# A second group norm in two chains of two channel blocks each, placed among the projection and Gram matmuls

## The reference

```python
hn = group_norm(x, gn1_scale, gn1_bias)              # 32 groups of 16 channels
... # layer 0: 8 heads of attention over 1024 positions -> a
out = jnp.einsum('bchw,oc->bohw', a, w_proj) + b_proj[None, :, None, None]
out = group_norm(out, gn2_scale, gn2_bias)
x1 = x + out                                          # input of layer 1
...
qkv = jnp.einsum('oc,bcn->bon', w_qkv, x1)            # weight-normed
rms = jnp.sqrt(jnp.mean(jnp.square(qkv), axis=1, keepdims=True)) + 0.0001
q, k, v = jnp.split(qkv / rms, 3, axis=1)
attn = softmax(einsum('bci,bcj->bij', q, k) * C ** (-0.5))
h = einsum('oc,bcn->bon', w_out, einsum('bij,bcj->bci', attn, v))
return (x1 + h) * 2.0 ** (-0.5)
```

## Time and profile before

| what | value |
|---|---|
| runs, median (lowest to highest) | 3598.97 us (3598.38 to 3599.15) |
| span of the profiled execution | 3596.4 us |
| mean granted TensorE clock in it | 0.984 |
| busy: TensorE, DVE, ScalarE, GpSimd | 97%, 59%, 51%, 28% |
| chain that ended last: TensorE, issue, DVE, ScalarE, GpSimd | 86%, 7%, 3%, 2%, 1% |

### The profile page before, as it was taken

How to read it: one execution, slowest core, us unless ns; L and a number is a source line. 1 busy time by engine, 2 the same in 40 slices (tenths; PEclk the granted TensorE clock), 3 DMA queues, 4 the chain that set the end, 5 groups by cost and what they waited for, 6 DMA issues and landing times.

```text
span 3596.4 us, 52422 instructions
## 1 busy us (share of the span) xinstructions
PE 3475.9 (97%) x17296; PEld 2845.8 (79%) x17296; DVE 2104.1 (59%) x3363; ACT 1828.4 (51%) x3082; POOL 994.2 (28%) x891
## 2 busy tenths in 40 slices
PE   7999999989999899998999989999999999999999
PEld 3887788878888788887878878788787887888878
DVE  4677446774378634786347854478444774447742
ACT  3577226761278522784237832388223882247812
POOL 0234103440034300352114521045111451114411
PEclk9999999999999999999999999999999999999999
DMA  7622215312234113331033211342203422142210
GB/s 278 180 45 65 91 38 139 78 41 82 65 112 95 48 59 95 86 91 71 36 118 83 71 71 42 112 95 60 82 36 106 95 60 82 39 135 62 59 47 24
DMA packets 63519, 294.41 MB, mean 82 GB/s; under 512 B 9200, under 2 KB 9456, under 8 KB 52464
## 3 DMA queue, kind: packets, MB, share of 16 engines
q1 hardware_dynamic: 63216, 290.65, 27.6%
HBM read 158.49 MB, written 31.46 MB: 53 GB/s over the span
## 4 chain that ended last, share of the span: by engine, by line
PE 86%; issue 7%; DVE 3%; ACT 2%; POOL 1%; DMA 0%; ACTq 0%; SPq 0%; DVEq 0%; POOLq 0%
PE big L419 36%; PE tps L516 14%; PE big L543 12%; PE ops L529 12%; PE ops L658 10%; DVE XA L1163 1%; PE ops L419 1%; ACT PB L784 1%; PE big L581 1%; POOL XA L912 1%; DVE HL L1284 0%; DVE small L1104 0%; PE big L635 0%; PE ops L624 0%; ACT RB L801 0%
## 5 line engine op out<-in xcount | busy, mean ns | idle before, releaser
L902 POOL TENSOR_SCALAR PB<-PB,small 128x1024 f32<-128x1024 f32 x576 | 647.9, 1125 | 1334.5 <-DVE small L1110 1328.6
L790 ACT ACTIVATE PT<-tps 128x512 fp32r<-128x512 f32 x1088 | 601.1, 597 | 249.4 <-PE tps L516 246.0
L1115 DVE TENSOR_TENSOR PT<-tps,PT 128x512 fp32r<-128x512 f32 x1088 | 692.7, 678 | 38.6 <-ACT PT L790 38.6
L419 PE MATMUL big<-HH,W 128*128 128x512 f32 x1856 | 618.2, 404 | 61.8 <-DVE HL L1284 56.5
L1104 DVE TENSOR_REDUCE small<-big 128x1 f32<-128x1024 f32 x512 | 624.7, 1220 | 62.5 <-PE big L543 59.2
L516 PE MATMUL tps<-ident,PB 128*128 128x128 f32 x4608 | 617.4, 275 | 8.4 <-DVE PT L1115 6.1
L516 PEld LDWEIGHTS tps<-ident,PB 128*128 128x128 f32 x4608 | 527.6, 140 | 122.0 <-DVE PT L1115 52.5
L784 ACT ACTIVATE PB<-big,small 128x1024 f32<-128x1024 f32 x512 | 572.2, 1117 | 73.1 <-DVE small L1104 70.2
L529 PE MATMUL ops<-PT,VT 128*128 128x512 f32 x2048 | 599.1, 414 | 0.0
L543 PE MATMUL big<-ST 128*128 128x512 f32 x2048 | 555.2, 393 | 10.9 <-ACT PB L784 10.9
L419 PEld LDWEIGHTS big<-HH,W 128*128 128x128 f32 x1856 | 361.8, 195 | 149.2 <-issue 70.9
(11 more groups left out here) (130 smaller groups left out, 3669.9 us busy)
## 6 DMA issues: line engine op xcount, KB each, us to landing
ST<-ST SPq DMA_DIRECT2D x384, 256.0 KB, 5.0
W<-d_qk SPq DMA_DIRECT2D x32, 1024.0 KB, 5.5
XA<-in_x SPq DMA_DIRECT2D x8, 2048.0 KB, 8.9
X<-in_x SPq DMA_DIRECT2D x8, 2048.0 KB, 10.4
W<-d_wp SPq DMA_DIRECT2D x8, 2048.0 KB, 12.1
W<-d_g SPq DMA_DIRECT2D x8, 2048.0 KB, 12.1
W<-d_m SPq DMA_DIRECT2D x8, 2048.0 KB, 7.8
W<-d_u SPq DMA_DIRECT2D x8, 2048.0 KB, 7.6
```

What stands on the lines that cost most here:

```text
L419: last = mm(dst, stat(sp_, k), mov(mp_, k), start=(i == 0), stop=(i == n - 1))
L790: act_fn(pt_slot(u, s)[:, 0, :], tps[n % 2][:], ACT.Copy).then_inc(s_pt_hi, 1)
L902: nc.gpsimd.tensor_scalar(PB[:, i, :], PB[:, i, :], rinv[:, i:i + 1], 1.0, ALU.mult, ALU.mult)\
L1115: V.tensor_tensor(pt_slot(u, s)[:, 1, :], tps[n % 2][:], pt_slot(u, s)[:, 0, :].bitcast(f32), ALU.subtract).then_inc(s_pt_ready, 1)
```

## The change

- Group norm 2 goes in two chains, of blocks 0 and 1 and of blocks 2 and 3. The first one's group matmuls stand inside projection 2 on TensorE (after 9 and after 15 of its 24 matmuls), the second one's inside Gram blocks 1 and 2. They write the small PSUM tiles tps, so "gna" and "gnb" of this norm leave `BIG`.
- DVE's, ScalarE's and GpSimd's programs are reordered to match: residual, high half, float32 copy and low half of a pair follow its chain, in whole blocks.
- GpSimd multiplies x by 1/sqrt(2) in place in four steps during attention (after steps 20, 23, 26, 29); gs2 is scaled once, and the scale disappears from the later steps.
- DVE makes the low half from XA, coefB and the high half, and no longer from GpSimd's copy.
- The Gram blocks are taken in pieces: what needs x1 blocks 0 and 1 first, then blocks 2 and 3. Three additions of products move from DVE to GpSimd.
- x1's blocks 0 and 1 go to ST, since HH and HL are still read by the projection; y's blocks go where there is room.

The core of the diff:

```diff
-BIG += [("proj", k) for k in range(KB)] + [("gna", 0), ("gnb", 0)] + [("g", k) for k in range(KB)]
+BIG += [("proj", k) for k in range(KB)] + [("g", k) for k in range(KB)]
+X_SCALE_STEPS = (20, 23, 26, 29)
...
-                    sp.wait_ge(s_xc_hi, (b + 1) * len(XC_PARTS))
+                    sp.wait_ge(s_xc_lo, (b + 1) * KB)
...
-                for o in (2, 3):
-                    project_out(released(("proj", o)), o, range(PAIRS)).then_inc(s_big_full, 1)
-                group_means(2 * b + 2, released(("gna", 0)), bp, s_big_full)
-                group_vars(2 * b + 2, released(("gnb", 0)), s_big_full)
+                t = released(("proj", 2))
+                project_out(t, 2, range(3), (0,))
+                gn2_means(0)
+                project_out(t, 2, [3], (0,))
+                project_out(t, 2, range(1), (1,))
+                gn2_vars(0)
+                project_out(t, 2, range(1, PAIRS), (1,)).then_inc(s_big_full, 1)
+                project_out(released(("proj", 3)), 3, range(PAIRS)).then_inc(s_big_full, 1)
...
-                for k in range(KB):
-                    from_x1("g", k, 0, range(k + 1))
+                x1_block(0)
+                from_x1(released(("g", 0)), 0, 0, (0,)).then_inc(s_big_full, 1)
+                t = released(("g", 1))
+                from_x1(t, 1, 0, (0,))
+                gn2_means(1)
+                x1_block(1)
+                from_x1(t, 1, 0, (1,)).then_inc(s_big_full, 1)
+                g2 = released(("g", 2))
+                from_x1(g2, 2, 0, (0,))
+                gn2_vars(1)
+                from_x1(g2, 2, 0, (1,))
+                g3 = released(("g", 3))
+                from_x1(g3, 3, 0, (0, 1))
+                x1_block(2)
+                from_x1(g2, 2, 0, (2,)).then_inc(s_big_full, 1)
+                from_x1(g3, 3, 0, (2,))
+                x1_block(3)
+                from_x1(g3, 3, 0, (3,)).then_inc(s_big_full, 1)
... ScalarE
+                out_f32(0)
+                out_f32(1)
+                xc_hi(0)
+                out_f32(2)
+                xc_hi(1)
+                out_f32(3)
+                xc_hi(2)
+                xc_hi(3)
... GpSimd
+                    nc.gpsimd.tensor_scalar(X[:, k, :], X[:, k, :], RES, 1.0, ALU.mult, ALU.mult)\
+                      .then_inc(s_x_scaled, 1)
...
+                for c in range(GN2_PARTS):
+                    rows = slice(2 * c, 2 * c + 2)
+                    group_rstd(GN_PER_BATCH * b + 2 + c, rows)
+                    pool.wait_ge(s_coef_b, b * GN2_PARTS + c + 1)
+                    for k in (2 * c, 2 * c + 1):
+                        pool.wait_ge(s_res_sum, b * KB + k + 1)
+                        nc.gpsimd.tensor_scalar(X[:, k, :], XA[:, k, :], 1.0, coefB[:, k:k + 1], ALU.mult, ALU.add)\
+                          .then_inc(s_xc_ready, 1)
+                for k in range(1, KB):
+                    pool.wait_ge(s_prod_ready, b * KB + k + 1)
+                    nc.gpsimd.tensor_tensor(PB[:, 4, :], PB[:, 4, :], PB[:, 4 + k, :], ALU.add)\
+                      .then_inc(s_prod_add if k < KB - 1 else s_prod_sum, 1)
... DVE
+                def xc_lo(k):
+                    dve.wait_ge(s_xc_hi, b * KB + k + 1)
+                    V.scalar_tensor_tensor(x1(1, k), XA[:, k, :], coefB[:, k:k + 1], x1(0, k).bitcast(f32),
+                                           ALU.add, ALU.subtract).then_inc(s_xc_lo, 1)
...
+                out_stats(0)
+                out_stats(1)
+                gn2_mean(0)
+                gn2_dev(0)
+                gn2_veps(0)
+                gn2_coefs(0)
+                residual(0)
+                out_stats(2)
+                residual(1)
+                xc_lo(0)
+                out_stats(3)
+                gn2_mean(1)
+                xc_lo(1)
+                gram_product(0)
+                gn2_dev(1)
+                gram_product(1)
+                gn2_veps(1)
+                gn2_coefs(1)
+                residual(2)
+                residual(3)
+                xc_lo(2)
+                xc_lo(3)
+                gram_product(2)
+                gram_product(3)
```

More of the change, by code:

```diff
@@ L74 @@
 BIG_BASE = SETUP_BIG
-DVE_LINKS = 16
+DVE_LINKS = 18
 SCALE0 = float(CH) ** -0.5
 SCALE1 = float(C) ** -0.5
-XC_PARTS = [(0, slice(0, HALF)), (0, slice(HALF, N))] + [(k, slice(0, N)) for k in range(1, KB)]
+GN2_PARTS = 2
+GN_PER_BATCH = GN2_PARTS + 1
+X_SCALE_STEPS = (20, 23, 26, 29)
 LAG = 5
@@ L571, in body, with project_out @@
                 pe.wait_ge(s_a_lo, b * 6 + 6)
-                def project_out(t, o, pairs):
-                    for half in range(2):
+                def project_out(t, o, pairs, halves=(0, 1)):
+                    for half in halves:
                         if o == 0 and pairs == [PAIRS - 1]:
@@ L599, in from_x1 @@
+                project_out(t, 2, range(3), (0,))
[5 more added lines that the diff above has]
+                project_out(released(("proj", 3)), 3, range(PAIRS)).then_inc(s_big_full, 1)
+                def from_x1(t, k, slot, blocks):
                     for half in range(2):
[L600 to L603, removed]
@@ L604, in from_x1 @@
                         cols = slice(HALF * half, HALF * half + HALF)
-                        last = split_product(t[:, cols], lambda h, j: w_full[slot][:, h, j, P * k:P * k + P],
-                                             lambda h, j: (HH, HL)[h][:, j, cols], blocks)
-                    last.then_inc(s_big_full, 1)
+                        for j in blocks:
+                            for i, (wp, xp) in enumerate(((0, 0), (0, 1), (1, 0))):
+                                last = mm(t[:, cols], w_full[slot][:, wp, j, P * k:P * k + P], x1(xp, j)[:, cols],
+                                          start=(j == 0 and i == 0), stop=(j == (k if slot == 0 else KB - 1) and i == 2))
@@ L833, in body, with out_f32 @@
                 a_hi(3, 1)
-                for o in range(KB):
+                def out_f32(o):
                     t = full(("proj", o))
@@ L1023, in channel_stats, with group_dev, group_veps, group_coefs @@
                 return V.bn_aggr(mv[:, k, :], stats[:, k, :])
[L1025 to L1033, removed]
+            def group_dev(means, mean, rows):
+                link(V.tensor_tensor(dev[:, rows], mean, means, ALU.subtract))
+                V.tensor_copy(gmean[:, rows], means)
+                V.tensor_tensor(dev[:, rows], dev[:, rows], dev[:, rows], ALU.mult).then_inc(s_gn_var, 1)
+            def group_veps(variances, rows):
+                V.tensor_scalar(veps[:, rows], variances, GN_EPS, None, ALU.add).then_inc(s_gn_veps, 1)
+            def group_coefs(n, scale, bias, rows):
                 dve.wait_ge(s_gn_rstd, n)
-                link(V.tensor_tensor(coefA, rstd, scale, ALU.mult))
-            def group_coef_b(bias, times):
-                link(V.scalar_tensor_tensor(coefT, gmean, times, coefA, ALU.mult, ALU.mult))
-                return V.tensor_tensor(coefB, bias, coefT, ALU.subtract)
+                link(V.tensor_tensor(coefA[:, rows], rstd[:, rows], scale[:, rows], ALU.mult))
+                link(V.tensor_tensor(coefT[:, rows], gmean[:, rows], coefA[:, rows], ALU.mult))
+                return V.tensor_tensor(coefB[:, rows], bias[:, rows], coefT[:, rows], ALU.subtract)
+            every = slice(0, KB)
             def norm_f32():
@@ L1141, in body, with out_stats @@
                      .then_inc(s_a_lo_last, 1)
-                for k in range(KB):
+                def out_stats(k):
                     dve.wait_ge(s_proj_half, b * 4 + k + 1)
```

176 lines of the change are left out of this document (94 added, 82 removed).

## The result

The changed kernel takes 3532.34 us (median of 4 runs, 3531.65 to 3532.79); the kernel before took 3598.98 beside it. The ratio is 0.9816, 95% interval 0.9802 to 0.983: 1.8% faster. The profiled execution has a span of 3529.9 us, 66.5 less, and a mean granted clock of 0.998, against 0.984.

What follows compares the result with a forecast made beforehand. TensorE, busy 97%, was bound to lose time only between last projection and Gram matmuls. Gain 8.5, less 1.4 for clock and 0.2 for scaling, is 6.9 us a batch, 55 in all: 3544 us, range 3522 to 3566.

Steps and rivals of the forecast that it cites:

- the first rival: Clock holds through the short Gram-stage idle time: 3533 us; with DVE ahead of GpSimd as well, 3524; together chance 0.25.
- What bounds the kernel: Between last projection and Gram matmuls: 13.8 us a batch lost to TensorE's idleness and half-speed clock.
- First chain: Inside projection 2: 8.9 us between projection and Gram work close to nothing, for 1.0 us of small matmuls.
- Wait of 0.7 us ahead of Gram block 1: TensorE idles 0.7 us while ScalarE copies out projection 3's tile, which Gram block 1 uses.
- Second chain: Inside Gram blocks 1 and 2: TensorE runs out at 366.9 and idles 2.7 us for block 2's low half.
- Turns of DVE and GpSimd: GpSimd's queued copy of block 2 excludes DVE's low half; with DVE first, idle 1.7 us and gain 9.5.
- The clock: After the 2.7 us idle, clock falls in three batches of four, at about 1.8 us: 1.4 us a batch.
- The sentence on the Trainium skill's warning: The skill warns only of idle gaps longer than 2.7 us; by that rule the time is 3533 us.
- Scaling x: In attention, scaling after step 26 delays step 27's normalise and TensorE's load: 0.2 us a batch, ends 0 and 0.4.
- Sums on GpSimd and the other parts at nothing: Three additions on GpSimd hidden by 4 us; fused scaling, tile places and renumbered counts put no work on the path.
- Sum: Per batch 8.5 - 1.4 - 0.2 = 6.9 us, over 8 batches 55 us: 3544 us; chance 0.51.

Runs made afterwards that it cites:

- e2: Changed kernel with GpSimd's copy of block 2 held until DVE's low half is done, plus two unused DVE row reductions lengthening TensorE's idle time: 3547.1 us.
- e3: Changed kernel with only the first chain's group matmuls put back behind projection 3, DVE's and ScalarE's order to match: 3612.66 us.
- e8: Changed kernel with the second chain's group matmuls moved behind the last Gram matmul that needs only blocks 0 and 1: 3584.19 us.
- e1: Changed kernel with one wait added: GpSimd's float32 copy of x1 block 2 waits until DVE's low half of block 2 is done: 3521.14 us.
- e5: Changed kernel with x scaled after steps 21, 23, 25 and 29 in place of 20, 23, 26 and 29: 3533.54 us.
- e6: Changed kernel with the three additions of products back on DVE, behind product 3: 3532.33 us.
- e7: Changed kernel with e1's wait, e4's early variances and e5's scaling steps together: 3512.61 us.
- e4: Changed kernel with the second chain's variance matmuls 6 matmuls earlier and DVE's read of them ahead of product 1: 3523.36 us.
- e2b: Like e2 with one more unused DVE row reduction (two of 1024 columns and one of 520), for about 3.7 us idle: 3560.07 us.

## Why the prediction was right, and where a term was off

The range held the time (3532.3 in 3522 to 3566) and so did the direction; the time is that of the first rival with the clock up, 3533, and not the forecast's 3544. That it falls so near to 3533 is luck: the rival has an idle time of 2.7 us in every image, and at such a length the clock fell in half of e2's images. The changed kernel came to the same time by a shorter wait (0.9 us an image less), one fall and a first image that is 4.1 us late. Step by step:

- **What bounds the kernel.** Right, though the two parts that the prediction named, 4.6 us idle and 4.5 of clock, are only 9.1 of its 13.8; the rest is mostly idle time ahead of 359.2 (3.1 us), which its 8.9 us between projection and Gram work include. With the first chain back behind the projections (e3) all of the gain and 14 us more are gone; with the second one late (e8) 52 of the 66 us are.
- **First chain.** Right: nothing is idle between projection 3 and the Gram matmuls, and the first low half is done 11.3 us after projection 2's start (11.9 expected), TensorE is there after 11.95 (12.0 expected); Gram block 0 follows the projection without a wait. The group matmuls cost 0.37 us a pair and not 0.5, and the projection stretch got 12.21 - 11.30 = 0.91 us longer for them and what they interrupt (1.0 expected).
- **Wait of 0.7 us ahead of Gram block 1.** It came, at 0.15.
- **Second chain.** The mechanism held, the wait was mis-sized: 1.8 in place of 2.7. It ended 1.0 us earlier. The power over two columns takes 0.70 us where the 1.77 us came from one over four (1.02), so the read-to-residual step is 1.45: 0.3 us. The start of that step was expected 19.3 us after projection 2's start and came 18.9 on: 0.4 us, from the cheaper group matmuls and the short wait. The rest, 0.2 us, is the stretch from residual(2) to TensorE's restart, 4.6 us in place of 4.8. Against this TensorE ran dry 0.1 us earlier than expected.
- **Turns of DVE and GpSimd.** Right: 4.10 us for two low halves beside the copies, 2.48 with GpSimd held back (e1). What the turns cost TensorE is 0.74 us an image, not 1.0. This pair of runs agrees with the rule of the Trainium skill (SBUF — State Buffer, "Who interferes with whom") that such a pair of instructions shut each other out.
- **The clock.** This is the term that failed: 1.4 us an image forecast, 0.2 measured (one fall of 1.6 in eight images). It failed through the length of the idle time and hardly through its price: at 2.8 us (e2) the time is 3547, 26 us above e1, as expected at the prediction's price, though the profiled execution of e2 has four falls in eight images and not six. The sentence on the Trainium skill's warning (TensorE: Matmul & The Clock Gate, "HAM oscillation — how this bites in real kernels") gave the time that came, 3533, but not for the reason it gives: idle gaps shorter than it warns of did lower the clock, four of the eight of 2.8 us in e2's trace and 15 in 32 of the 1.8 us ones. Here the measurement decides.
- **Scaling x.** Right in place, 0.3 us in place of 0.2 in size. In image 1 the timelines of GpSimd and of TensorE's loads show the answer to the earlier trace rows: the scaling, step 27's normalise behind it, and the load that waits for it.

```profile
646.08 1.05 POOL L981 TENSOR_SCALAR X<-X 128x1024 f32<-128x1024 f32 x1
647.23 1.14 POOL L962 TENSOR_SCALAR PB<-PB,small 128x1024 f32<-128x1024 f32 x1
...
648.49 0.85 PEld L532 LDWEIGHTS tps<-ident,PB 128*128 128x128 f32 x8 [0.52 <-DVE PT L1193]
```

  The normalise ends at 648.37 and the load comes 0.1 later. The profile names DVE's line 1193 for the load, which ends just then too; but of the two only the normalise has moved against the steps around it, by 1.0 us. Up to step 28 the score matmuls keep their distances of before, from step 30 on they come 0.3 us later (0.2 forecast); with the scaling at other steps this is gone (e5).
- **Sums on GpSimd and the other parts at nothing.** Right (e6). The three additions took 3.36, 2.40 and 2.38 us and ended 5.7 us ahead of the column sums.
- **Sum.** Forecast 6.9 us an image: 8.5 with the clock up, less 1.4 and 0.2. Measured 9.3 (the stage's 10.0 and 0.2 for the one fall, less 0.9 for the longer projection stretch), less 0.2 and 0.3: 8.8; the 0.8 more in the first term is the wait that was 0.9 shorter. The same by stretches: 10.0 for the stage, less 1.2 for the longer rest: 8.8, or 70.6 in all, less 4.1 us of a late first image (5.3 at line 395, of which 1.2 are the longer rest), which no term foresaw.

The last is only partly explained. In image 0 TensorE waited 2.5 us for the DMA that stacks the first head, after the weights' store in setup had landed later. That wait is 0.5 to 2.3 us in the traces of all the experiments but e7, where it is absent; e7 holds all parts of the change and reached line 395 at 354.64. The one trace of the kernel before has none. So the change doesn't bring it every time, and whether it makes it likelier stays open, as does why it varies. A difference of 2 or 3 us between two kernels' times can come from it; the lengths of stages and stretches can't.

## What to carry to other kernels

A chain of small steps between two dense stages is hidden by cutting the data, not the steps: half of the channels' chain fits under the matmuls that end the one stage, the other half under those of the next that need only the first half, and here either half's place was worth most of the gain (80 and 52 us against 66; the two don't add up to the gain). Each long wait that stayed cost its idle time and some of the slow clock behind it. Take the durations of the new chain from rows of its new shape where there are any, and follow the engines that slow each other, here DVE and GpSimd: a copy that isn't needed yet and is queued too early cost 0.74 us an image, as much as one chain's small matmuls (2 x 0.37). And an edit that saves 2 us can be worth nothing while a wait that lowers the clock in some images and not in others is left in every one (e5 had five falls for one); remove that wait first (e7).

## What the runs showed of the hardware that was not expected

- The granted clock after an idle time is not decided by its length alone. Idle times of 1.1 and 1.2 us lowered it in no image of e1 and e4 (16), those of 1.8 us in 15 of 32 (the changed kernel, e3, e5, e6), those of 2.8 us in 4 of 8 (the fastest of e2's executions), those of 3.8 us in 8 of 8 (e2b). The same kernel with the same wait can have a fall in one image and none in the next.
- A fall lasted between 3.4 us (changed kernel) and 13.7 us (the kernel before); it cost 1.4 to 2.9 us an image in e2 and e2b, and no more than about 3 us in e8, where its 10.2 us began inside the long idle time.
- GpSimd's power of two columns took 0.70 us and of four 1.02 (both in the changed kernel), so the number of columns matters even there.
- An addition of 128x1024 on GpSimd took 2.39 us undisturbed, twice DVE's 1.22, and 3.36 where it began beside DVE's low half.
